# GraphSAGE layers in split fp32r: how the tile means reach the centring in the first layer

## The reference, cut to what matters

```python
h = maximum(layernorm(x, eps=1e-5), 0)            # x is 10000 x 512, no gain, no shift
def sage_conv(x, Wp, bp, Wl, bl, Wr):             # 5000 edges src -> dst, dst sorted
    h = relu(x @ Wp.T + bp)
    agg = segment_sum(h[src], dst) / maximum(count(dst), 1)
    return agg @ Wl.T + bl + x @ Wr.T
def relu_ln(x, g, b): ...                         # relu, then layer norm with gain g and shift b
out = x + conv2(relu_ln(conv1(relu_ln(conv0(h)))))
```

## Time and profile before

| | |
|---|---|
| median of 3 runs | 1548.34 us (1545.14 to 1548.49) |
| profiled execution | 1544.51 us, its span (first to last instruction) 1542.8 us |
| busy share of the span | PE 96%, PEld 77%, DVE 69%, ACT 46%, POOL 40% |
| mean granted TensorE clock | 0.995 |
| chain that ended last | PE 77%, DVE 10%, issue 7%, DMA 4%, ACT 2% |

### The profile page before, as it was taken

One profiled execution on the slowest core, in us unless ns is written; L12 is line 12 of the kernel. 1 busy time (PEld: TensorE's weight loads), 2 busy tenths in 40 slices (PEclk: granted clock), 3 DMA queues, 4 the chain that ended last, 5 costly groups with the idle time before them and its releaser, 6 DMA issues.

```text
span 1542.8 us, 20850 instructions
## 1 busy us (share of the span) xinstructions
PE 1483.1 (96%) x6953; PEld 1193.7 (77%) x6953; DVE 1061.7 (69%) x2217; ACT 706.5 (46%) x1376; POOL 624.2 (40%) x533
## 2 busy tenths in 40 slices
PE   5889987999999999999999999999999999999999
PEld 4666665788887788888878888888888887888887
DVE  8989997877775677777565655557776756555552
ACT  3545423444442577766422323257676742323321
POOL 2894426476642200100244443225455464444321
PEclk9999999999999999999999999999999999999999
DMA  9899966455554588878555455479999984545545
GB/s 309 321 325 298 269 206 209 133 97 90 89 90 68 137 286 287 284 268 282 190 155 89 84 93 89 65 178 345 357 380 348 375 284 122 88 89 89 90 62 143
DMA packets 160326, 299.46 MB, mean 194 GB/s; under 512 B 23517, under 2 KB 23708, under 8 KB 160092
## 3 DMA queue, kind: packets, MB, share of 16 engines
q1 hardware_dynamic: 129900, 232.51, 43.9%
q0 software_dynamic: 29744, 64.57, 24.1%
q10 hardware_dynamic: 576, 1.05, 0.2%
HBM read 158.56 MB, written 139.40 MB: 193 GB/s over the span
## 4 chain that ended last, share of the span: by engine, by line
PE 77%; DVE 10%; issue 7%; DMA 4%; ACT 2%; POOL 0%; SPq 0%; DVEq 0%; ACTq 0%; POOLq 0%
PE bank L889 10%; PE bank L890 9%; PE bank L891 9%; PE bank L866 8%; PE bank L987 7%; PE bank L985 7%; PE bank L986 7%; PE bank L966 7%; PE bank L965 7%; PE bank L964 7%; DMA xn<-x_t 3%; DVE h_low L1267 2%; DVE stats L1286 2%; DVE xn L1312 1%; DVE rows_out L1409 1%
## 5 line engine op out<-in xcount | busy, mean ns | idle before, releaser
L889 PE MATMUL bank<-w_high,h_low 128*128 128x512 f32 x876 | 367.3, 419 | 17.5 <-DVE h_low L1267 14.7
L890 PE MATMUL bank<-w_low,h_high 128*128 128x512 f32 x876 | 348.2, 398 | 0.0
L891 PE MATMUL bank<-w_high,h_high 128*128 128x512 f32 x876 | 347.7, 397 | 0.0
L1175 ACT ACTIVATE h_high<-h_pre 128x500 fp32r<-128x500 f32 x120 | 74.6, 622 | 363.4 <-DVE h_pre L1561 363.4
L889 PEld LDWEIGHTS bank<-w_high,h_low 128*128 128x128 f32 x876 | 166.6, 190 | 62.4 <-DVE h_low L1267 26.2
L891 PEld LDWEIGHTS bank<-w_high,h_high 128*128 128x128 f32 x876 | 166.8, 190 | 40.6
L964 PE MATMUL bank<-xt_low,w_high 128*128 128x500 f32 x480 | 195.2, 407 | 1.5 <-issue 1.5
L985 PE MATMUL bank<-w_high,h_low 128*125 128x512 f32 x480 | 190.5, 397 | 1.9 <-DVE h_low L1567 1.9
L1270 DVE TENSOR_TENSOR h_low<-bank,h_high 128x512 fp32r<-128x512 f32 x146 | 100.6, 690 | 132.4 <-ACT h_high L1120 125.7
L890 PEld LDWEIGHTS bank<-w_low,h_high 128*128 128x128 f32 x876 | 166.8, 190 | 30.4
L987 PE MATMUL bank<-w_high,h_high 128*125 128x512 f32 x480 | 190.0, 396 | 0.0
(11 more groups left out here) (139 smaller groups left out, 2545.8 us busy)
## 6 DMA issues: line engine op xcount, KB each, us to landing
rows_in<-node_z SPq DMA_DIRECT2D x158, 256.0 KB
node_x<-xn SPq DMA_DIRECT2D x158, 256.0 KB, 3.7
node_z<-rows_out SPq DMA_DIRECT2D x142, 256.0 KB
out<-rows_out SPq DMA_DIRECT2D x79, 256.0 KB
rows_in<-x SPq DMA_DIRECT2D x78, 256.0 KB
residual<-x SPq DMA_DIRECT2D x78, 256.0 KB, 5.0
xn<-x_t SPq DMA_DIRECT2D x71, 256.0 KB
node_z<-bias_z SPq DMA_DIRECT2D x16, 256.0 KB
```

The source lines that it names most:

```text
L889: nc.tensor.matmul(psum, low[:, k, :], w_high("r", l)[:, k, :], start=(k == 0), stop=False)
L890: nc.tensor.matmul(psum, high[:, k, :], w_low("r", l)[:, k, :], start=False, stop=False)
L891: last = nc.tensor.matmul(psum, high[:, k, :], w_high("r", l)[:, k, :], start=False, stop=(k == K - 1))
```

## The change

Four edits. First, ScalarE copies the means of one tile from `mean_rows` to `mean_flat`, where the 128 means lie next to each other (a ring of 2), and the centring of tiles 20 to 70 reads from there. Second, the diagonal is made once, in fp32, by ScalarE alone; VectorE's part and the semaphore for it go, and TensorE does one fp32 matmul with fp32 ones. Third, the diagonals lie in `h_pre` instead, so the first late one waits for the last `h_low`. Fourth, 20 matmuls of ones by ones into bank 7, whose result is not used, stand ahead of TensorE's work; GpSimd no longer makes an fp32r copy of the ones. SP's load of a later group's means waits for ScalarE's copies instead of the centring.

```diff
+WARM = 20
-        diag_high, diag_low = (flat_of(b, 0)[:, 2 * K * P:(2 * K + DIAGS) * P].rearrange("p (r c) -> p r c", r=DIAGS)
-                               for b in (h_high, h_low))
+        diag = h_pre[:, 0, 0:DIAGS * P].rearrange("p (r c) -> p r c", r=DIAGS)
+        mean_flat = sb("mean_flat", [P, 2, P], F32)
...
-                            sp.wait_ge(n_centred, 4 * (g - 1))
+                            sp.wait_ge(n_flat, 4 * (g - 1) - BY_PE)
...
+            pe.wait_ge(ones_done, 1)
+            for _ in range(WARM):
+                nc.tensor.matmul(bank[7][:, 0:P], ones[:], ones[:], start=True, stop=True)
...
-                pe.wait_ge(n_diag_low, d + 1)
-                psum, slot = bank[c % 2][:, 0:P], d % DIAGS
-                nc.tensor.matmul(psum, ones_r[:], diag_low[:, slot, :], start=True, stop=False)
-                nc.tensor.matmul(psum, ones_r[:], diag_high[:, slot, :], start=False, stop=True).then_inc(turned, 1)
+                pe.wait_ge(n_diag, d + 1)
+                nc.tensor.matmul(bank[c % 2][:, 0:P], ones[:], diag[:, d % DIAGS, :], start=True, stop=True
+                                 ).then_inc(turned, 1)
...
                 if late == 0:
-                    act.wait_ge(e_product, EDGE_TILES - GROUP)
-                S.activation(diag_high[:, slot, :], ident[:], ACT.Identity, scale=minus_mean[:, t:t + 1]
-                             ).then_inc(n_diag_high, 1)
+                    act.wait_ge(e_h_low, EDGE_TILES)
+                S.activation(diag[:, slot, :], ident[:], ACT.Identity, scale=minus_mean[:, t:t + 1]
+                             ).then_inc(n_diag, 1)
+
+            def flat_mean(t):
+                g, n = t // 4, t - BY_PE
+                act.wait_ge(mean_loaded[g % 2], DMA * ((g - BY_PE // 4) // 2 + 1))
+                if n >= 2:
+                    act.wait_ge(n_centred, t - 1)
+                S.activation(mean_flat[:, n % 2, :], mean_rows[g % 2][:, :, t % 4], ACT.Identity).then_inc(n_flat, 1)
...
                         for t in first_at(i, AHEAD_DIAG):
                             if t < BY_PE:
-                                diag_high_of(t)
+                                diag_of(t)
+                            else:
+                                flat_mean(t)
...
-                    g = t // 4
-                    dve.wait_ge(mean_loaded[g % 2], DMA * ((g - BY_PE // 4) // 2 + 1))
-                    centre(xn[:, t % XN_RING, :], mean_rows[g % 2][:, :, t % 4])
+                    dve.wait_ge(n_flat, t - BY_PE + 1)
+                    centre(xn[:, t % XN_RING, :], mean_flat[:, (t - BY_PE) % 2, :])
```

More of the change, by code:

```diff
@@ L136, in sage_kernel @@
         shift_sum = sb("shift_sum", [P, D], F32)
-        ones_f = sb("ones_f", [P, P], F32)
-        ones_r = sb("ones_r", [P, P], F32R)
-        ones = ones_r[:].bitcast(F32)
+        ones = sb("ones", [P, P], F32)
         ident = sb("ident", [P, P], F32)
@@ L281, in sage_kernel @@
         n_scale = sem("n_scale")
-        n_diag_high = sem("n_diag_high")
-        n_diag_low = sem("n_diag_low")
+        n_diag = sem("n_diag")
+        n_flat = sem("n_flat")
         n_centred = sem("n_centred")
@@ L692, in _ @@
             G.memset(eps[:], EPS).then_inc(eps_done, 1)
-            G.memset(ones_f[:], 1.0).then_inc(ones_done, 1)
+            G.memset(ones[:], 1.0).then_inc(ones_done, 1)
             pool.wait_ge(ones_done, 1)
-            G.affine_select(out=ident[:], in_=ones_f[:], compare_op=ALU.is_equal, fill=0.0, base=0,
+            G.affine_select(out=ident[:], in_=ones[:], compare_op=ALU.is_equal, fill=0.0, base=0,
                             pattern=[[1, P]], channel_multiplier=-1).then_inc(ident_done, 1)
-            G.tensor_scalar(ones_r[:], ones_f[:], 1.0, None, ALU.mult).then_inc(ones_done, 1)
             G.memset(dst_i[:], PAD_NODE).then_inc(pads_done, 1)
@@ L869, in spread_mean @@
             def spread_mean(c, d):
-                if c == 0:
-                    pe.wait_ge(ones_done, 2)
                 if c >= 2:
                     pe.wait_ge(xt_low_done, c - 1)
-                pe.wait_ge(n_diag_low, d + 1)
-                psum, slot = bank[c % 2][:, 0:P], d % DIAGS
-                nc.tensor.matmul(psum, ones_r[:], diag_low[:, slot, :], start=True, stop=False)
-                nc.tensor.matmul(psum, ones_r[:], diag_high[:, slot, :], start=False, stop=True).then_inc(turned, 1)
+                pe.wait_ge(n_diag, d + 1)
+                nc.tensor.matmul(bank[c % 2][:, 0:P], ones[:], diag[:, d % DIAGS, :], start=True, stop=True
+                                 ).then_inc(turned, 1)
             def node_turn(l, t):
@@ L1070, in root_of, with diag_of @@
                 S.activation(spread[:, t:t + 1], mean[:, u % IN_RING, 1:2], ACT.Sqrt, bias=eps[:]).then_inc(n_root, 1)
-            def diag_high_of(t):
+            def diag_of(t):
                 slot, late = diag_no(t) % DIAGS, t - product_count[0]
@@ L1243, in _ @@
                     for j in late_turns(l, s) if l == 0 else ():
-                        diag_high_of(product_count[0] + j)
+                        diag_of(product_count[0] + j)
                     for j in late_turns(l, s):
@@ L1299, in minus_of @@
                                 ).then_inc(n_minus, 1)
[L1301 to L1306, removed]
             def centre(rows, minus):
@@ L1604, in _ @@
                             node_xt_low(l, t)
-                        for t in first_at(i, AHEAD_DIAG):
-                            if t < BY_PE:
-                                diag_low_of(t)
                         for k in R_CHUNKS.get(i, ()):
@@ L1659, in _ @@
                         edge_factors(edge_norms_beside(s))
-                        for j in late_turns(l, s):
-                            diag_low_of(product_count[0] + j)
                         for j in late_turns(l, s):
```

## The result

The changed kernel takes 1533.72 us (median of 4 runs, 1533.32 to 1536.93), the one before, run beside it, 1547.76 us (4 runs). The ratio is 0.9917, with a 95% interval of 0.9899 to 0.9935: 14 us faster, where 19.5 were forecast. One of the runs of the kernel before that belong to the first experiments took 2962.84 us in a slow state, and no ratio uses it.

| | before | after | gain so far |
|---|---|---|---|
| step 0 | 23.18 | 20.93 | 2.3 |
| step 20 | 99.07 | 95.11 | 4.0 |
| step 51 | 201.76 | 194.39 | 7.4 |
| step 70 | 276.19 | 268.17 | 8.0 |
| L944, at the end of the edge stage | 518.52 | 509.55 | 9.0 |

The account below looks back on a forecast made before the run. From 94 to 204 us VectorE, with the DMA it waits for, was taken as the bound, TensorE next; 4 + 10.5 + 1 + 2.5 + 1.5 = 19.5 us off the median 1548.3 gives 1528.8 us, range 1519 to 1540.

Parts of the forecast that it names:

- The centring and the copy: Tiles 20 to 70: centring 0.36 us less a tile, bounds 0 and 0.40; ScalarE's copy 0.45 us, bounds 0.34 and 0.48, hidden.
- Rival (d): The gaps cost nothing: centring stays at 0.96 us, only the diagonals pay, 5.5 us, 1543; chance 0.04.
- (c): ScalarE now holds the wait for the means' load, delaying VectorE and TensorE: 13 us slower, 1561; chance 0.04.
- The middle: 94 to 204 us: shorter centrings gain 11.9 us, turned tile loads take 1.4 back; 10.5 us, bounds 5 and 15.8.
- rival (a): Turned tile loads take the centring's place; start, late diagonals and fuller steps pay 4 + 1.5 + 4 = 9.5 us, 1539; chance 0.2.
- The start: Before 94 us: cheaper diagonals on VectorE and earlier GpSimd masks gain 4 us, bounds 1.5 and 6.3.
- The stall and 213 to 265 us: Stall at 206 us stays, softened: 1 us, bounds 0 and 5.3; 213 to 265 us: 2.5 us, bounds 0.5 and 5.
- The late diagonals: 501 to 519 us: the first of a pair ready 0.4 us sooner, four times; 1.5 us, bounds 0.5 and 1.6.
- the fp32 matmuls: Diagonals on TensorE: one fp32 matmul replaces two; 0 us taken, bounds 0 and 5.6 us more.
- The warm-up: Twenty matmuls from the first microsecond, expected to end near 8 us: cost 0, bounds -1 and +2.

Follow-up runs that it names:

- the first experiments: First occasion of follow-up runs: changed kernel again, only the means' copy, and a fifth turned-tile buffer on both kernels; the kernel before took 1546.19 us there.
- the kernel with the fifth buffer: Changed kernel with five instead of four first-layer buffers for turned tiles, each load issued one step earlier: 1522.59 us, ratio 0.9855 to the kernel before.
- the second time: The changed kernel run again without any edit, beside the kernel before: 1532.74 us, ratio 0.9913.
- the means out of the way: Changed kernel with a fifth turned-tile buffer and the means' store and broadcast at the end of SyncE's step: 1518.25 us, ratio 0.9816 to the kernel before.
- both orders: Changed kernel, fifth turned-tile buffer, means' store and broadcast at SyncE's step end, turned tile's load ahead of the row store: 1516.35 us, ratio 0.9801 to the kernel before.
- the flat copy alone: Kernel before with only ScalarE's copy of the means and the centring from it; diagonals in two halves, no warm-up: 1537.27 us, ratio 0.9946.
- the diagonal alone: Changed kernel with the means' copy undone; full-precision diagonals and warm-up stay: 1542.11 us, ratio 0.9969 to the kernel before.
- either order alone: Changed kernel, four buffers, means' store and broadcast at SyncE's step end: 1532.23 us, 0.9916; or turned tile's load ahead of row store: 1529.87 us, 0.9912.
- before + fifth buffer: Kernel before with a fifth buffer for turned tiles in the first layer and each load issued one step earlier: 1537.70 us, ratio 0.9949.

## Why the prediction was right or wrong

**The centring and the copy: right.** The next instruction starts after 0.58 us, for the forecast 0.60, and where VectorE catches up behind a late load its steps are 2.58 us, as 2.97 - 0.38 should give. ScalarE's copy takes 0.416 us, between the bounds, and hides. Rival (d) falls. So does (c): ScalarE waited 3.0 us for means, in 4 waits of at most 1.0. Its mechanism shows only in the kernel with the fifth buffer, with 20.5 us of such waits, where it eats a gain and makes nothing slower.

**The middle, 10.5 us forecast: this term was mis-sized.** The two traces of the changed kernel show 3.4 and 2.6 us from step 20 to 51. The 31 centrings of this stretch are shorter as forecast, by 0.36 us each that makes 11.2 us, but VectorE's waits for turned tiles grow there from 2.7 us in 3 waits to 10.8 us in 9 (11.6 in 9 the second time). The difference, 8.1 us, leaves 3.1. The prediction named this wait as the next one, gave a load 5.5 us and let the growth cost 1.4 us: it took the waits before as the ones that grow, by 0.35 to 0.7 us each. In fact loads that nobody waited for before are late too, since each load is issued once a step's rows are out, and a shorter step shortens its lead: 6.2 us before, 5.6 after (median), and 4.2 in the chain above. Its landing of 5.88 us would have fitted into the old lead. That is rival (a), which priced the fuller steps at 4 us. The fifth buffer shows that it is this bound: with it on both sides the change gives 5.4 us there (99.7 to 94.3), and with the means out of the way 8.5 to 10.0 (to 91.2 and 89.7), about what was forecast, though the kernel before was not run with the means moved. With the fifth buffer and both orders 31 steps take 89.7 us, 2.89 each, near the 2.79 that TensorE needs. So the bound that the prediction expected is reached only there.

**The start, 4 us forecast: the size right, partly by luck.** Step 20 comes 4.0 us earlier (4.1 the second time). But 2.3 of it is there at step 0, where the first diagonals are ready sooner (with the flat copy alone step 0 gains nothing). The masks start 2.7 us earlier (23.77 after 26.46 us) and end 6.7 earlier, where 1.5 and 4.5 were estimated; not all of it arrives, because a turned tile's load is late by 3.42 us right ahead of step 20. With the loads cured step 20 comes at 89.9 us.

**The stall and 213 to 265 us, 1 + 2.5 us:** steps 51 to 70 gained 0.7 us in one trace and 3.8 in the other. VectorE's waits for loads grew from 4.8 to 8.0 us in this stretch. The stall stays, and which instruction is held changes with the execution; in the first trace the low half lasts 5.93 us beside 4.94 us of GpSimd. The Trainium skill (SBUF — State Buffer, SBUF: two separate sides) has the two engines lock each other out of a shared pair of ports; the trace agrees. Spread, the subtractions held VectorE as long in sum, so no run shows what lifting the lock would bring.

**The late diagonals, 1.5 us:** 0.95 us from step 70 to L944 (242.33 to 241.38), 0.95 also with the diagonal alone, and 0.1 with the flat copy alone. One pair gains 0.35 us: its matmul starts 0.53 us behind ScalarE instead of 0.92 (508.10 to 509.02 before), and the centring then 0.56 behind that instead of 0.52. TensorE waits for three of the four pairs and not, as forecast, for all four: before, the first pair's matmul (504.62) has no wait ahead of it. So the fp32 matmuls cost next to nothing, as taken, though the prediction misread a row for it: 519.03 lies 0.51 us behind the start of the first pass of L944 (518.52), not behind both passes.

**The warm-up, 0 us:** nothing that could be measured, 1533.4 beside 1532.7 us, with overlapping intervals of the ratio.

**The sum.** The terms come to 4.0 + 3.4 + 0.7 + 0.95 = 9 us in the first trace and 4.1 + 2.6 + 3.8 + 0.9 = 11.4 in the second, and the medians say 13.5 to 14.0. The remaining 2 to 5 us can't be given a place, with one trace of the kernel before, whose execution was 3.3 us under its median. Against the forecast of 19.5 the median misses by 5.5 us, of which the middle is 7.1 to 7.9 too high (some 0.7 less by the 31 centrings of the stretch measured, the forecast having 33), and the rest goes the other way. By the 9 us of the first trace alone the time would have been 1539 us, at the edge of the range of 1519 to 1540.

## What to carry to other kernels

When a step is to get shorter, list the lead of each transfer, from its issue to the time at which it is wanted, as it will be with the new step, and compare it with the landing times that the waits show; do not count only the transfers that someone waited for before. A queue that holds a wait on a small store delays everything behind it, but here its removal paid only once a fifth buffer had been added; test such cures together as well as one by one. Here one more buffer was worth 10 us and either order alone nothing. And when an edit is to remove a stall, look in its trace whether the stall is gone before its time is read.

## What the runs showed of the hardware

The warm-up did not keep TensorE's clock up. Busy from 1.09 to 8.04 us, TensorE had a granted clock of 0.50 (1.2 GHz) from 13 to 15 us, after 3.33 us of idling, and again from 23 to 26 us, after 2.09 us, with starts 0.43 us apart (columns: length, busy us, clock, DMA share, GB/s):

```profile
13.00:15.00 2.00, 2.00 (x6) 0.50 1.05 400
...
23.00:26.00 3.00, 2.96 (x8) 0.50 0.94 278
```

Without it nine starts of the first product are 0.43 us apart too, the later ones 0.23, also from 23 us on, and the recorded clock was 1.00 up to 208 us: there the record and the spacing disagree.

The stall costs TensorE more than its idle time. In the second trace of the changed kernel it idled 3.08 us up to 207.55; from 208.63 us on its matmuls start 0.43 us apart, with a granted clock of 0.50 from 209 to 211 us.

Four back to back subtractions on GpSimd held one VectorE instruction with two operands in SBUF for nearly all their 4.9 to 5.0 us (5.93, 4.44 and 5.47 us in three traces, depending on where it began). In two traces ("before + fifth buffer" and "diagonal and warm-up only") the two engines took turns instead: the four took 6.4 us, the longest VectorE instruction 2.14 and 2.07 us, and TensorE idled 1.98 and 1.96 us. What decides between the two is not shown. In "diagonal and warm-up only":

```profile
204.47 6.37 POOL L721 TENSOR_TENSOR w_low<-stage,w_high 128x512 fp32r<-128x512 f32 x4
204.61 1.75 DVE L1275 SCALAR_TENSOR_TENSOR h_low<-xn,h_high 128x512 fp32r<-128x512 f32 x1
...
207.62 2.07 DVE L1313 TENSOR_TENSOR xn<-xn,residual 128x512 f32<-128x512 f32 x1
```

With a gather between the subtractions the longest centring was 2.34 us. A cast with one operand was held as well, 1.93 us instead of 0.19.

A 2 KB store of means took 5.07 us to land, hardly less than the 256 KB load with 5.88, while DMA moved 306 GB/s in the mean from 90 to 190 us.
